# Four row buffers and a new spacing for the sorted tiles, and overflow passes placed inside other work

## The reference

```
ys = y * scale
out = (Efou * ys) @ weight * d                      # conditioned projection: xf
top1 = argmax(softmax(xf @ gate_w.T))               # one of 2 experts per token
routing = relu(masked @ w1 + b1) @ w2 + b2, summed over both experts
shared  = relu(xf @ sw1 + sb1) @ sw2 + sb2
x = x + (routing + shared)
```

## Time and profile before

| | us |
|---|---|
| median of three runs | 1457.22 (1457.13 to 1457.71) |
| the profiled execution | 1471.43 |
| its span, first to last instruction | 1469.7 |
| PE busy | 1390.4 |
| DVE busy | 904.7 |
| ACT busy | 642.5 |
| POOL busy | 282.6 |

### The profile page before, as it was taken

How to read it: one execution, slowest core, us unless ns; L and a number is a source line. 1 busy time by engine, 2 the same in 40 slices (tenths; PEclk the granted TensorE clock), 3 DMA queues, 4 the chain that set the end, 5 groups by cost and what they waited for, 6 DMA issues and landing times.

```text
span 1469.7 us, 17093 instructions
## 1 busy us (share of the span) xinstructions
PE 1390.4 (95%) x6086; PEld 1146.9 (78%) x6086; DVE 904.7 (62%) x1313; ACT 642.5 (44%) x929; POOL 282.6 (19%) x260
## 2 busy tenths in 40 slices
PE   9999999998899657999899999999999999999995
PEld 8888888887688445788788888888888887888884
DVE  7979978584796321867357787877784443333331
ACT  4455645453466332566567444444553221222220
POOL 0000006322222232200000000001001222055665
PEclk9999999999999878899999999999999999999998
DMA  6957584977998446773357797979898756366653
GB/s 211 311 181 243 193 265 163 262 249 268 302 303 258 158 155 191 258 205 109 125 187 257 247 291 247 285 249 310 289 277 297 200 148 155 90 187 165 165 128 59
DMA packets 223925, 317.65 MB, mean 216 GB/s; under 512 B 51440, under 2 KB 98544, under 8 KB 223824
## 3 DMA queue, kind: packets, MB, share of 16 engines
q1 hardware_dynamic: 200528, 267.06, 55.9%
q0 software_dynamic: 22016, 47.00, 12.9%
q10 hardware_dynamic: 1296, 2.49, 0.5%
HBM read 184.47 MB, written 140.90 MB: 221 GB/s over the span
## 4 chain that ended last, share of the span: by engine, by line
PE 84%; DMA 6%; issue 4%; POOL 2%; DVE 2%; ACT 1%; SPq 0%; ACTq 0%; POOLq 0%; DVEq 0%
PE bank L1852 38%; PE bank L1922 21%; PE bank L1951 18%; PE bank L1780 6%; DMA loose_rows<-x_rows,tab_in 3%; POOL loose_rows L847 1%; POOL out L833 1%; DMA hidden_scratch<-vb 1%; DMA rows<-sorted_scratch 1%; DMA sorted_scratch<-sorted_rows 1%; PE bank L1875 1%; DVE rows L1331 0%; DMA hidden_scratch<-vt 0%; DVE vb L1400 0%; DMA loose_rows<-loose_rows,loose_at 0%
## 5 line engine op out<-in xcount | busy, mean ns | idle before, releaser
L1852 PE MATMUL bank<-xw,w_hi 128*128 128x512 f32 x1792 | 561.3, 395 | 58.1 <-ACT vb L990 36.5
L1852 PEld LDWEIGHTS bank<-xw,w_hi 128*128 128x128 f32 x1792 | 340.8, 191 | 132.6 <-issue 34.5
L1367 DVE TENSOR_TENSOR hl<-hin,hl 128x512 fp32r<-128x512 f32 x352 | 236.5, 688 | 264.1 <-ACT hl L966 263.3
L966 ACT CAST hl<-hin 128x512 fp32r<-128x512 f32 x352 | 216.7, 621 | 385.1 <-PE bank L1951 223.6
L1852 PE MATMUL bank<-xw,w_lo 128*128 128x512 f32 x896 | 352.7, 394 | 0.0
L1951 PE MATMUL bank<-w_hi,hl 128*128 128x512 f32 x1024 | 315.9, 390 | 1.3 <-DVE res_u L1702 1.3
L1922 PE MATMUL bank<-hl,w_hi 128*128 128x512 f32 x896 | 276.0, 390 | 0.0
L1951 PEld LDWEIGHTS bank<-w_hi,hl 128*128 128x128 f32 x1024 | 192.3, 188 | 41.5 <-issue 1.7
L1951 PE MATMUL bank<-w_lo,hl 128*128 128x512 f32 x512 | 199.4, 390 | 0.0
L1852 PEld LDWEIGHTS bank<-xw,w_lo 128*128 128x128 f32 x896 | 170.8, 191 | 35.8
L1922 PEld LDWEIGHTS bank<-hl,w_hi 128*128 128x128 f32 x896 | 168.3, 188 | 34.8
(11 more groups left out here) (184 smaller groups left out, 1197.0 us busy)
## 6 DMA issues: line engine op xcount, KB each, us to landing
hin<-hidden_scratch SPq DMA_DIRECT2D x112, 512.0 KB, 4.6
hidden_scratch<-vb SPq DMA_DIRECT2D x80, 512.0 KB, 4.2
hin<-expert_hidden SPq DMA_DIRECT2D x64, 512.0 KB, 4.5
expert_hidden<-vb SPq DMA_DIRECT2D x48, 512.0 KB, 3.8
hidden_scratch<-vt SPq DMA_DIRECT2D x32, 512.0 KB, 4.4
w_new<-w_shared SPq DMA_DIRECT2D x52, 256.0 KB, 5.9
sorted_scratch<-sorted_rows POOLq DMA_DIRECT2D x48, 256.0 KB, 4.4
ring<-x_cols SPq DMA_DIRECT2D x32, 256.0 KB, 5.1
```

The costliest lines, as they stand in the source:

```text
L966: nc.scalar.copy(hl[:, n % HL, 0, :], hin[:, n // 2 % LOADS, n % 2, :]).then_inc(hu_hi, 1)
L1367: nc.vector.tensor_tensor(hl[:, n % HL, 1, :], hin[:, n // 2 % LOADS, n % 2, :], hl[:, n % HL, 0, :].bitcast(F32), ALU.subtract).then_inc( ...
L1852: last = nc.tensor.matmul(up_bank(u, UP_BANK[c])[p][:], w[:, DOWN_W[c], pair, part], xw[:, c, x, k, :], start=(c in FRESH and n == 1), sto ...
```

## The change

The sort gets four buffers instead of two. The gather of tile k now waits for the store of tile k - 4, and the store of tile k is issued after the gather of tile k + 2 instead of k + 1. The thresholds in `up_mm` are no longer 140 + 2k: the first eight tiles stand 3 products apart, the next eight 4, all others 2, so tile 7 may start at 161, tile 16 at 196, tile 47 at 258. ACT's wait at group 20 is now for all 48 tiles, not for the first 32 of the order. The overflow rows of the expert down stage get four buffers too, with the same semaphores; the order of POOL's instructions there is the same.

In `loose_up` PE multiplies three quarters into banks 4, 5 and 6 as soon as step 3 of the group has been added, turns the first, multiplies the fourth, and turns the rest into banks 2 and 3. It no longer waits for ACT's last relu. ACT's loads of the next overflow rows move behind the relus. `loose_down` moves from ahead of wide unit 3 to ahead of its step 8, writes to a bank of the unit before, and PE's wait for DVE at its end becomes a wait ahead of wide unit 4.

```diff
 SORT = (*range(KD * W), *range(NT, COLS), *range(KD * W, NT))
+SORT_PACE = (3, 4, 2, 2, 2, 2)
-LOOSE_DOWN = 3
+LOOSE_DOWN = (3, 8)
...
-        sorted_rows = [at(kb, f"sorted_rows{i}", [D]) for i, kb in enumerate((208, 210))]
+        sorted_rows = [at(kb, f"sorted_rows{i}", [D]) for i, kb in enumerate((208, 210, 212, 214))]
...
-        loose_banks, loose_turned = banks[0:QUADS], banks[QUADS:QUADS + 2]
+        loose_banks, loose_turned = banks[QUADS:2 * QUADS], banks[2:4]
...
-                pool.wait_ge(up_mm, PER_GROUP * SORT_GROUP + 2 * k)
-                wait(pool, sorted_out[k % 2], DMA * (k // 2))
+                i, u = k % RING, SORT[k]
+                pool.wait_ge(up_mm, PER_GROUP * SORT_GROUP + sum(SORT_PACE[j // 8] for j in range(k)))
+                wait(pool, sorted_out[i], DMA * (k // RING))
...
-            for k in range(COLS):
-                sort_in(k)
-                if k > 0:
-                    sort_out(k - 1)
-            sort_out(COLS - 1)
+            for k in range(COLS + 2):
+                if k < COLS:
+                    sort_in(k)
+                if k >= 2:
+                    sort_out(k - 2)
...
-                i, u = k % 2, NT + k
-                wait(pool, loose_rows_out[i], DMA * (k // 2))
+                i, u = k % RING, NT + k
+                pool.wait_ge(sorted_out[i], DMA * ((COLS + k) // RING))
...
-                        for i in range(2):
-                            act.wait_ge(sorted_out[i], DMA * ((SORT.index(COLS - 1) + 1) // 2))
+                        for i in range(RING):
+                            act.wait_ge(sorted_out[i], DMA * COLS // RING)
...
+                for q in range(QUADS - 1):
+                    flat(q)
+                take(0)
+                flat(QUADS - 1)
+                for q in range(1, QUADS):
+                    take(q)
+                act.wait_ge(loose_lo, 2 * x + 2)
+                loose_rows_load(x + 1)
...
-                pe.wait_ge(loose_relu, HC * (x + 1))
+                pe.wait_ge(loose_lo, 2 * x + 2)
+                pe.wait_ge(up_added, 6 * u + 2)
+                for q in range(QUADS - 1):
+                    products(q)
+                pe.wait_ge(up_added, 6 * (u + 1))
+                turn_back(0)
+                products(QUADS - 1)
+                for q in range(1, QUADS):
+                    turn_back(q)
...
-                pe.wait_ge(loose_sum, 2 * x + 2)
...
+                if wide == LOOSE_DOWN[0] + 1:
+                    pe.wait_ge(loose_down_done, 2)
```

More of the change, by code:

```diff
@@ L273, in build @@
         res = [at(kb, f"res{i}", [D]) for i, kb in enumerate((176, 178, 180, 182))]
-        loose_rows = [at(kb, f"loose_rows{i}", [D]) for i, kb in enumerate((164, 166))]
+        loose_rows = [at(kb, f"loose_rows{i}", [D]) for i, kb in enumerate((164, 166, 200, 202))]
         bias = aux
@@ L318, in build @@
         b2_in = sem("b2_in")
-        sorted_in = [sem(f"sorted_in{i}") for i in range(2)]
-        sorted_out = [sem(f"sorted_out{i}") for i in range(2)]
+        sorted_in = [sem(f"sorted_in{i}") for i in range(RING)]
+        sorted_out = [sem(f"sorted_out{i}") for i in range(RING)]
         xr_in = [sem(f"xr_in{i}") for i in range(XR)]
@@ L426, in build @@
         loose_down_done = sem("loose_down_done")
-        loose_rows_in = [sem(f"loose_rows_in{i}") for i in range(2)]
-        loose_rows_out = [sem(f"loose_rows_out{i}") for i in range(2)]
         def read_split(eng):
@@ L544, in raw_load @@
                 if n == RAW_LAST:
-                    for i in range(2):
-                        sp.wait_ge(sorted_out[i], DMA * COLS // 2)
+                    for i in range(RING):
+                        sp.wait_ge(sorted_out[i], DMA * COLS // RING)
                 if n == RAW_LAST + 1:
@@ L577, in next_rows @@
                     tiles_done = SORT.index(W * 2 * (s + 2 - BLOCKS) - 1) + 1
-                    sp.wait_ge(sorted_out[0], DMA * (tiles_done // 2))
-                    sp.wait_ge(sorted_out[1], DMA * (tiles_done // 2))
+                    for i in range(RING):
+                        sp.wait_ge(sorted_out[i], DMA * (tiles_done // RING))
                 if s * GROUPS == LOOSE_UP[0] and q == 0:
@@ L750, in _ @@
                 sp.wait_ge(scattered[i], DMA * UNITS_E)
-            for i in range(2):
-                sp.wait_ge(loose_rows_out[i], DMA * (CAP // P // 2))
+            for i in range(RING):
+                sp.wait_ge(sorted_out[i], DMA * ((COLS + CAP // P) // RING))
         @block.gpsimd
@@ L1066, in loose_up, with flat @@
             def loose_up(e, x):
-                for q in range(QUADS):
+                def flat(q):
                     act.wait_ge(loose_clear, e + 1)
@@ L1071, in loose_up, with take @@
                     nc.scalar.copy(hq[0:S, q, :], loose_banks[q][0:S, :]).then_inc(loose_flat, 1)
-                act.wait_ge(loose_lo, 2 * x + 2)
-                loose_rows_load(x + 1)
-                for q in range(QUADS):
+                def take(q):
                     act.wait_ge(loose_back, QUADS * x + q + 1)
@@ L1863, in loose_up, with products @@
             def loose_up(u, x):
-                pe.wait_ge(loose_lo, 2 * x + 2)
-                for q in range(QUADS):
-                    if q == 0:
-                        pe.wait_ge(up_added, 6 * (u + 1))
-                        pe.wait_ge(up_kept, 8 * (u + 1))
+                def products(q):
                     pairs = slice(W * (q % 2), W * (q % 2) + W)
@@ L1877, in loose_up, with turn_back @@
                     last.then_inc(loose_mm, 1)
-                for q in range(QUADS):
+                def turn_back(q):
                     pe.wait_ge(loose_folded, QUADS * x + q + 1)
```

54 lines of the change are left out of this document (27 added, 27 removed).

## The result

The changed kernel takes 1421.33 us (median of 4, 1419.77 to 1422.89) against 1457.47 for the kernel before, measured with it (median of 4, 1457.13 to 1460.28): a ratio of 0.9748, 95% interval 0.9729 to 0.9767. It is 36 us faster. The forecast was 57 us, and its range, 1385 to 1413, misses the time by 8.

What follows compares the result with a forecast made beforehand. PE's matmul stream was taken as the bound, with some 79 us of holes. Gains 8.7 + 26.9 + 19.3 + 1 + 1.2 = 57.1 off the 1457.2 median gave 1400.1 us, range 1385 to 1413.

Steps and rivals of the forecast that it cites:

- A: PE's loss before group 20's third step, 15.7 us: 7 taken as staying, between 0 and 15.7, gain 8.7.
- B: PE's hole at group 20, 31.9 us, ACT waiting for sorted tiles: 5 taken as staying, gain 26.9.
- C: After group 20, block 6's rows waiting for 40 sorted tiles: the wait goes whole, gain 19.3 us.
- overflow pass, up stage: Pass and groups behind it, 17.3 us lost: ACT still waits for its stores, gain 1 us, between 0 and 7.2.
- down stage to the end: In the down stage's overflow pass the 1.29 us wait for DVE goes, gain 1.2 us; the tail adds 0.
- The gain is up to that much less: Warning: if profiling slowed transfers, the 14.2 us between profiled and timed executions could come off the gain.
- Against it stands slack: In A: `vt1`'s store may take 9.8 us and takes 4.4, absorbing some 4 to 5 us once.
- the tail: POOL's chain from output tile 12 to the last scatter, 180 to 182 us as before: gain 0, at most 1.
- Half to POOL: Rival, 14%: POOL's full queue takes half the transfers; A becomes a loss of 19, B vanishes, 1413 us.
- The wait for 48 tiles: Rival, slower, 3%: four buffers don't speed the sort, group 20 waits 107 us, 1511; decided at 5.7 us a tile.

Runs made afterwards that it cites:

- its copy: The kernel before, unchanged, run and profiled a second time: 1458.82 us beside 1458.98, ratio 1.0007; the profiled execution took 1458.36 us.
- the third look: The kernel before, unchanged, profiled once more: one run of 1466.57 us beside 1463.36 for seven of the same kernel.
- the passes alone: The kernel before with only the new overflow passes, `loose_up` and `loose_down`: 1454.62 us, ratio 0.9957.
- the quiet sort: Changed kernel with ACT's wait split (32 tiles, then 48) and ten tiles sorted early, then none until group 14: 1413.86 us, ratio 0.9684.
- half of the rows: Changed kernel loading only half of block 4's rows, so its results are not the reference's: 1415.39 us, ratio 0.9716.
- the experiment on the last stage: Changed kernel with the last stage's adding gather two tiles behind its gather and the scatter three: 1419.97 us, ratio 0.9731.

## Why the prediction was wrong

Its own terms, in us. The columns are what was lost in the first trace of before, in the second one (the 1456.6 us span), in after, and then the gain as predicted and as measured against the first and the second trace. Group 20's third step ideally comes 386.5 after the first matmul (97.93, 97.15, 97.5 in the three); PE stopped at 500.08, 495.6 and 497.5.

| term | before, 1st | before, 2nd | after | predicted gain | gain, 1st | gain, 2nd |
|---|---|---|---|---|---|---|
| A, before group 20 | 15.7 | 12.0 | 13.4 | 8.7 | 2.3 | -1.4 |
| B, group 20 and its clock | 31.9 | 22.5 | 8.4 | 26.9 | 23.5 | 14.1 |
| C, block 6's rows | 19.3 | 19.7 | 0 | 19.3 | 19.3 | 19.7 |
| overflow pass, up stage | 17.3 | 16.2 | 15.1 | 1.0 | 2.2 | 1.1 |
| down stage to the end | 678.0 | 679.6 | 677.0 | 1.2 | 1.1 | 2.6 |
| start | 97.9 | 97.2 | 97.5 | 0 | 0.4 | -0.3 |
| sum | | | | 57.1 | 48.8 | 35.8 |
| spans | 1469.7 | 1456.6 | 1421.1 | | 48.6 | 35.5 |

In the first two columns the slow clock behind group 20 stands in C, in the third in B; the sums are not touched by it. So of the miss of 21, some 8 us are in the terms and 13 in the trace that they were measured on. (The profiled execution of after, 1422.89, misses its own forecast of 1414.3 by 8.6.)

**The base.** The step that failed first is "Sum: ... against the median of 1457.2 it is 1400.1". It takes gains read as the size of holes in a run of 1471 off a median of 1457. The prediction saw the 14.2 us, said that no row explains them, and then left them out of the sum. The table shows where they were: A and B, 3.7 and 9.4 us. Both hang on the sort, a chain in which each gather waits for the landing of an earlier store, so that a small difference per tile adds up over some 30 tiles: 6.96 us a tile up to the 33rd gather in the first trace, 6.59 in the second. Why the two executions differ in that stays open. A gain that fills such a hole can't be larger than the hole in the runs it is compared with. "The gain is up to that much less" was the right warning, and should have been a term: with it and with A at no gain the range would have reached 1400.1 + 14.2 + 8.7 = 1423. Whether profiling itself slows the two-buffer sort stays open too: the profiled runs stood 14.2, -0.5, 3.2 and 9.2 us from the medians (before, its copy, the third look, the passes alone), those of the four-buffer kernels within 3.

**A.** "I take 7 us of A as staying" was 13.4, and against the second trace nothing was won at all. The first half of the reasoning held: SP no longer waits for sorted tiles, and the transfers themselves are what is late next. Where the loss sits, by the starts of every 84th matmul, in us beyond the 19.04 of a group:

| group | 5 | 13 | 14 | 15 | 16 | 17 | 18 |
|---|---|---|---|---|---|---|---|
| before, 1st | 0.5 | 6.6 | 8.1 | 0.0 | 0.7 | 0.0 | 0.0 |
| before, 2nd | 0.5 | 2.1 | 8.4 | 0.0 | 1.1 | 0.0 | 0.0 |
| after | 0.5 | 0.0 | 10.0 | 0.0 | 1.7 | 0.6 | 0.9 |

The change took away the loss of group 13 and left group 14's, which before had too and the prediction put down to SP's wait with the rest. The step that failed is "Against it stands slack": it counted the spare time of `vt1`'s store, 4 to 5 us, but the buffer that stopped PE was `vb21`, whose store stands in SP's order behind the weights and rows and took 4.91 us only to be issued. Nothing was absorbed: of the 10.0 us, 6.3 are this stop and 1.1 a second one at 389, the rest mostly the slow clock behind them (taken at 1 to 2). And groups 16 to 18 lost 3.2 where A had nothing; 1.1 of it is a stop at 415.5 for ACT and 0.5 one at 469.4 for DVE, what delayed those two was not followed.

The demand of group 13 itself was sized right, by luck. At the lengths of after's window its 1792 store, 1024 weight, 3072 row and some 440 sort packets take 422 us of engine time, and at the 437 that the window holds in 25 us this is 24.1 us, against 24.6. But 330 GB/s was a rate with row packets in it and no limit: groups 14 and 15, with no rows, need by the same lengths (an estimate) some 19 us each and not 21 to 22. Bytes price the rows at 4.8 us instead of 8.8, and everything else too high. The earlier trace rows gave the share, 1.09, beside the 345 GB/s: the share and the packets behind it were what to carry over to other groups, not the GB/s.

**B.** Predicted to stay 5, stayed 6.6 of stop plus 1.8 behind it (732 matmuls in 167.79 us instead of 165.9, with the window 500 to 525 at 0.86). The race of the last tile with group 20 was right: tile 47 stored at 497 and landed at 501.1, where 493 was expected (18 tiles at 4.2 and 13 at 3.0 give 490, so the prediction's own sum was 3 off), with PE ready at 497.5 instead of 491. The pace was 4.05 us a tile from tile 16 on ((490.62 - 364.98) / 31), where 3.0 to 4.2 was assumed. One row was misread on the way: the gather at 524.83 in the earlier trace rows is tile 32's, not tile 31's, since the store of tile 31 stands behind it, so before's pace was 6.96 us and not 7.19. It moves no term by over 2 us.

**C, the passes, the tail.** C went whole, and PE is busy 25.00 of 25 us in the window 575 to 600. The pass of the up stage behaved step by step as written. ACT and PE, against the earlier trace rows:

```profile
682.57 2.05 ACTq L1056 DMA_DIRECT2D soft<-sorted_scratch  x3
684.88 0.41 ACTq L1089 DMA_DIRECT2D loose_hidden<-hu  x1
685.74 0.37 ACTq L1090 DMA_DIRECT2D loose_hidden<-hu  x1
...
689.64 0.19 ACT L1114 COPY primed<-ones 128x1 f32<-128x1 f32 x1 [2.58 <-DMA loose_hidden<-hu]
```
```profile
690.50 0.74 PE L1860 MATMUL bank<-xw,w_hi 128*128 128x512 f32 x2 [3.27 <-ACT vb L990]
```

The stores still end it, and PE stands 3.27 us in its third step (4 forecast), released by ACT. The 1.29 of the earlier trace rows is gone. The tail stayed at "no gain" (180.6 us from output tile 12 to the last scatter, 180 to 182 forecast), and for the reason given: the buffers don't touch a wait of the add for its own gather; the experiment on the last stage shows that the order does.

**The rivals.** Half to POOL gave 1413 and was the nearest in time, but not in mechanism: it had A as a new loss of 19 to 25 and B gone. POOL's queue had 24.4 of 109 points of engine time in group 13 (above), and between 400 and 425, with its tiles 2 products apart, 36.3 beside SP's 64.4:

```profile
q1 hardware_dynamic: 3644, 5.99, 64.4%
q0 software_dynamic: 912, 2.97, 36.3%
```

That is a third of the time, not half. The rule of turns that the prediction quotes holds for queues that have work, and no window here is known to have both full throughout, so it is neither borne out nor refuted. The sign named for this rival, vt stores above 10 us in groups 13 to 17, can't be read in after, whose trace has no landings for them; between 350 and 400 their median was 6.3 us with the quiet sort and 7.8 with half of the rows (8.4 in before), but 15.1 for the two in the kernel with every tile as early as possible. So a faster sort can slow SP's stores, as that rival had it. The wait for 48 tiles decided nothing: the pace of 4.05 was far from 5.7.

## What to carry to other kernels

Read a hole's size in more than one execution before you book it as a gain, above all where it ends a chain of dependent transfers: here it was 22 to 32 us in three traces of one kernel, and the one nearest the median had the small one. Price transfers by the time they take of the transfer engines, packet by packet, and not by bytes. Count the slack of the store that stands last in its queue, and not of another. And before reordering a queue, ask if the queue or the sum is full: here two new orders of SP moved the stall to another buffer, while taking the sort's traffic out of the 37 us before group 14 removed it, and that was worth 15 us by the ratios (17 by the medians) with the wait and the last stage set right.

## What the runs showed of the hardware

Between 350 and 375 in after a packet of 512 bytes took 0.046 us of an engine's time and one of 2048 bytes 0.085; with about half as many of the small ones, 0.033 and 0.085. So full engines moved 403 GB/s with few of the small ones (350 to 355) and 192 with little else (361 to 366). In the stretch from 355 to 374 with the engines full, issuing itself stalled: four single transfers took SP 3.6 to 4.9 us each where 0.36 is the shortest, so that everything behind them in its order is late too. And a short stop is paid twice: after 6.6 us without a matmul the window 500 to 510 shows a granted clock of 0.66 (the lower of the two levels for part of it), and the 732 matmuls behind it took 1.9 us more than at the full clock.
